# A transformer block and an RWKV block on one core: both ends of the program rebuilt, and all turn numbers replaced

## The reference

```python
# layer 0 (16 heads of 16), per batch
qkv = layernorm(x) @ w_qkv + b_qkv;  x = x + attention(q, k, v, mask_self) @ w_ao + b_ao
q = layernorm(x) @ w_q + b_q;  k, v = split(enc @ w_kv + b_kv);  x = x + attention(q, k, v, mask_cross) @ w_co + b_co
x = x + gelu(layernorm(x) @ w1 + b1) @ w2 + b2
# layer 1 (32 heads of 8)
xn = ln(x); sx = token_shift(xn); xxx = tanh((xn + sx * maa_x) @ maa_w1) @ maa_w2
x5 = xn + sx * (maa_stack + xxx)                       # five mixed streams
w = exp(-exp(time_decay + tanh(x5[1] @ decay_w1) @ decay_w2))
r, k, v, g = x5[3] @ Wr.T, x5[0] @ Wk.T, x5[2] @ Wv.T, silu(x5[4] @ Wg.T)
# over the tokens, per head: out_t = r_t (u k_t v_t + s);  s = k_t v_t + w_t s
x = x + groupnorm(out) * g @ Wo.T
xn2 = ln(x); sx2 = token_shift(xn2)
x = x + sigmoid((xn2 + sx2 * fmr) @ Wr2.T) * (square(relu((xn2 + sx2 * fmk) @ Wk2.T)) @ Wv2.T)
```

## Time and profile before

| | |
|---|---|
| median of three runs | 681.06 us |
| profiled execution, its span | 682.92 us, 681.1 us |
| first instruction of VectorE | 1.00 us |
| busy share PE, PEld, DVE, ACT, POOL | 94%, 82%, 88%, 84%, 46% |
| mean granted TensorE clock | 0.989 |
| granted clock in 653 to 659 us, in 659 to 660 us | 0.50 to 0.51, 0.58 |
| chain that ended last, by engine | PE 69%, ACT 16%, DVE 8%, issue 4%, DMA 1%, POOL 1% |
| PE idle in 0 to 17, 17 to 34, 34 to 51, 51 to 68 us | 6.5, 2.6, 2.6, 1.7 us |
| PE idle in 68 to 150 us, in 150 to 550 us | 3.0 us, 2.1 us |
| PE idle in 550 to 600, 600 to 640, 640 to 681.1 us | 6.2, 4.2, 11.2 us |

### The profile page before, as it was taken

One profiled execution on the slowest core, in us unless ns is written; L12 is line 12 of the kernel. 1 busy time (PEld: TensorE's weight loads), 2 busy tenths in 40 slices (PEclk: granted clock), 3 DMA queues, 4 the chain that ended last, 5 costly groups with the idle time before them and its releaser, 6 DMA issues.

```text
span 681.1 us, 17297 instructions
## 1 busy us (share of the span) xinstructions
PE 641.1 (94%) x5877; PEld 559.5 (82%) x5877; DVE 599.8 (88%) x1430; ACT 569.1 (84%) x2069; POOL 310.2 (46%) x440
## 2 busy tenths in 40 slices
PE   6889999999999999999999999999999989798876
PEld 5667788898888888988888888889889878688665
DVE  3699589999999999999999999999999997977674
ACT  1678999899999999999999999999999988664612
POOL 1254362546464554636364645446363644432220
PEclk9999999999999999999999999999999989999979
DMA  9920040310404050503122130505040222502200
GB/s 345 296 73 10 2 120 21 111 32 17 125 24 118 1 141 1 140 10 97 45 87 63 39 103 3 140 1 141 1 131 12 79 62 63 148 1 63 78 9 8
DMA packets 55293, 50.44 MB, mean 74 GB/s; under 512 B 6062, under 2 KB 50982, under 8 KB 54822
## 3 DMA queue, kind: packets, MB, share of 16 engines
q1 hardware_dynamic: 55206, 49.34, 24.8%
HBM read 28.62 MB, written 3.93 MB: 48 GB/s over the span
## 4 chain that ended last, share of the span: by engine, by line
PE 69%; ACT 16%; DVE 8%; issue 4%; DMA 1%; POOL 1%; SPq 0%; DVEq 0%; ACTq 0%
PE PS_B L730 14%; PE PS_T L832 8%; PE PS_S L730 6%; ACT SC L1473 5%; PE PS_B L872 5%; PE PS_D L737 5%; PE PS_T L840 4%; PE PS_S L803 4%; PE PS_S L737 3%; PE PS_T L737 3%; ACT PT L1483 2%; PE PS_D L978 2%; PE PS_D L730 2%; PE PS_T L723 2%; PE PS_B L894 2%
## 5 line engine op out<-in xcount | busy, mean ns | idle before, releaser
L1473 ACT ACTIVATE SC<-SC,NMX 128x128 f32<-128x128 f32 x512 | 200.1, 400 | 1.6 <-DVE NMX L1157 1.4
L1473 ACT ACTIVATION_READ_ACCUMULATOR SC<-SC,NMX 128x1 f32 x512 | 102.0, 199 | 0.0
L832 PE MATMUL PS_T<-CST,SC 128*128 128x128 f32 x512 | 81.0, 281 | 10.5 <-ACT SC L1473 6.2
L1157 DVE TENSOR_REDUCE NMX<-SC 128x4 f32<-128x512 f32 x128 | 84.1, 668 | 2.9 <-POOL SC L1680 1.9
L1483 ACT ACTIVATE PT<-PS_T 128x512 f32<-128x512 f32 x120 | 71.3, 594 | 11.5 <-PE PS_T L832 9.7
L832 PEld LDWEIGHTS PS_T<-CST,SC 128*128 128x128 f32 x512 | 56.6, 142 | 28.4 <-ACT PT L1483 14.7
L1238 DVE TENSOR_TENSOR_SCAN SS<-W,AJ 128x1024 f32<-128x1024 f32 x32 | 73.1, 2286 | 2.4 <-DMA W<-EW 1.7
L730 PE MATMUL PS_B<-MX,W 128*128 128x128 f32 x512 | 64.8, 276 | 1.1 <-ACT KR L1532 1.0
L1680 POOL TENSOR_TENSOR SC<-SC,MADD 128x512 f32<-128x512 f32 x48 | 60.1, 1278 | 6.9 <-DVE SC L1137 6.7
L730 PEld LDWEIGHTS PS_B<-MX,W 128*128 128x128 f32 x512 | 60.7, 192 | 1.8 <-ACT KR L1532 1.2
L730 PE MATMUL PS_B<-B_LT,W 128*128 128x128 f32 x512 | 61.2, 278 | 0.5 <-ACT B_LT L1411 0.4
(11 more groups left out here) (229 smaller groups left out, 1622.0 us busy)
## 6 DMA issues: line engine op xcount, KB each, us to landing
W<-EW SPq DMA_DIRECT2D x32, 512.0 KB, 4.1
V<-values_by_head SPq DMA_DIRECT2D x28, 512.0 KB, 5.7
W<-in_weights SPq DMA_DIRECT2D x1, 4160.0 KB, 18.1
ENC<-in_enc SPq DMA_DIRECT2D x16, 128.0 KB, 3.7
out<-X SPq DMA_DIRECT2D x16, 128.0 KB, 4.4
values_by_head<-VC SPq DMA_DIRECT2D x14, 128.0 KB, 2.1
X<-in_x SPq DMA_DIRECT2D x1, 1664.0 KB, 22.4
W<-in_weights SPq DMA_DIRECT2D x1, 1280.0 KB, 8.6
```

Of the source, the lines that this page charges most:

```text
L832: last = pe.transpose(PS_T[:, j * T:(j + 1) * T], SC[:, nr(b, a) % 2, g, j, :], ident)
L1157: dve.tensor_reduce(NMX[:, nr(b, a) % 2, GH * g:GH * g + GH], SC[:, nr(b, a) % 2, g], AX_X, ALU.max, negate=True)\
L1473: last = act.activation(SC[:, nr(b, a) % 2, g, j, :], SC[:, nr(b, a) % 2, g, j, :], ACT.Exp, bias=NMX[:, nr(b, a) % 2, h:h + 1], accum_out ...
```

## The change

The diff has six parts, and one that runs through everything.

1. **First statistics.** The load of the tokens gets a semaphore of its own (`in_tokens`), and VectorE takes the statistics and moments of batch 0 as soon as they are there, ahead of the tables. GpSimd makes `SEL` later, in `b_root(0, 0)`.
2. **Products on zeros.** GpSimd clears 128 columns of `A_N` first of all, and TensorE makes six products of these zeros ahead of its first wait. The products of the identity in front of `a_turn(0, 0)` go from 4 to 2, the two in front of `a_val(0, 0)` now stand in front of `a_key(0, 0)`, and those in `d_out(14)`, `d_val(14)` and `d_read(15)` are left out (two each).
3. **First values in a free bank.** The values of batch 0 go to `PS_B`, and `a_scores(0, 0)` no longer waits for them; every `a_pv` does.
4. **Row copies later.** The ScalarE copies of two bias rows (L1466) move from the first exponentials to behind the sixth.
5. **Last decays.** For batches 14 and 15 ScalarE writes the exponentials straight into `W8`, eight times over, in two activations of 128x1016; `b_wspread` issues nothing for them. `d_scan` waits for one half at a time.
6. **Last values in a free bank.** The value product of batch 15 goes to `PS_T` and no longer waits for the copy of keys and receptance; the gate product does.
7. **New turn numbers** for all engines and batches.

```diff
+EARLY_WARM = 6
-    ('a_turn', 0, 0): 4, ('a_val', 0, 0): 2, ('a_prob_turn', (0, 0), 0): 8, ('a_prob_turn', (0, 1), 0): 4,
+    ('a_turn', 0, 0): 2, ('a_key', 0, 0): 2, ('a_prob_turn', (0, 0), 0): 8, ('a_prob_turn', (0, 1), 0): 4,
...
-    ("a_turn", 0, 5845), ("a_val", 0, 7302), ("a_key", 0, 7410), ("a_query", 0, 7948), ("a_scores", 0, 9532),
+    ("a_turn", 0, 5768), ("a_key", 0, 6952), ("a_val", 0, 7612), ("a_query", 0, 7784), ("a_scores", 0, 9446),
...
-            sp.dma_start(X[:, 0, :], x[0]).then_inc(in_first, 16)
+            sp.dma_start(X[:, 0, :], x[0]).then_inc(in_tokens, 16)
...
+            pe.wait_ge(set_zero, 1)
+            for _ in range(EARLY_WARM):
+                pe.matmul(PS_B[:, 0, 0:P], A_N[:, 0:P], A_N[:, 0:P], start=True, stop=True)
             pe.wait_ge(in_first, IN_FIRST)
...
-                pe.wait_ge(a_v, nr(b, a) + 1)
+                pe.wait_ge(a_v, nr(b, a) + 1 if later(b, a) else 0)
...
             def b_valgate(b, k):
                 if k:
+                    if b == B - 1:
+                        pe.wait_ge(b_kr, B)
                     to_channels(PS_B[:, 0, C:2 * C], "g", C, 0, MX[:, 4]).then_inc(b_vgps, 1)
-                else:
+                elif b < B - 1:
                     pe.wait_ge(b_kr, b + 1)
                     pe.wait_ge(b_mx, 3 * b + 3)
                     to_channels(PS_B[:, 0, 0:C], "v", C, 0, MX[:, 2])
+                else:
+                    pe.wait_ge(a_res, 2 * B)
+                    pe.wait_ge(b_mx, 3 * B)
+                    to_channels(PS_T[:, 0:C], "v", C, 0, MX[:, 2]).then_inc(b_vgps, 1)
...
+            dve.wait_ge(in_tokens, 16)
+            dve.bn_stats(A_ST[:, :], X[:, 0, :]).then_inc(a_stat, 1)
+            dve.wait_ge(a_stat, 1)
+            dve.bn_aggr(A_MV[:, :], A_ST[:, :]).then_inc(a_var, 1)
             dve.wait_ge(set_col, 1)
...
                 act.wait_ge(b_w8, 32 * b)
-                act.activation(EW[:, :, 1:T], DW[:, :, 0:T - 1], ACT.Exp, scale=-1.0).then_inc(b_ew, 1)
+                if b < B - LAST:
+                    act.activation(EW[:, :, 1:T], DW[:, :, 0:T - 1], ACT.Exp, scale=-1.0).then_inc(b_ew, 1)
+                else:
+                    act.wait_ge(d_s, 2 * b)
+                    for t in range(CT):
+                        step = DW[:, t, 0:T - 1].unsqueeze(1).to_broadcast([P, RS, T - 1])
+                        act.activation(W8[:, t, :, 1:T], step, ACT.Exp, scale=-1.0).then_inc(b_w8, 16)
...
+            pool.memset(A_N[:, 0:P], 0.0).then_inc(set_zero, 1)
             pool.wait_ge(in_first, IN_FIRST)
-            pool.tensor_copy(SEL[:, :, :].rearrange("p d (h i) -> p d h i", i=RS),
```

More of the change, by code:

```diff
@@ new lines @@
+    ("b_mlp1", 0, 35991), ("b_mlp1", 1, 36020), ("b_mlp2", 0, 36342), ("b_mlp2", 1, 36691), ("b_turn", 1, 38299),
+    ("b_low1", 0, 39134), ("b_low2", 0, 39900), ("b_low2", 2, 40700), ("b_decay1", 0, 41270), ("b_decay2", 0, 42125),
+    ("b_keyrec", 0, 42323), ("b_keyrec", 1, 42364), ("b_valgate", 0, 42963), ("b_valgate", 1, 43267),
+    ("b_select", 0, 43467), ("b_select", 1, 44943), ("d_own", 0, 50288), ("d_read", 0, 50868), ("d_oturn", 0, 51334),
+    ("d_biasout", 0, 54082), ("d_yturn", 0, 54513), ("d_out", 0, 55700), ("d_turn", 0, 56815), ("d_keyrec", 0, 58592),
@@ new lines @@
+    ("b_valgate", 1): {0: 42756, 2: 42204, 9: 43545, 10: 42838, 11: 41952, 12: 43205, 15: 41878},
+    ("b_select", 0): {14: 44665, 15: 42269}, ("b_select", 1): {14: 47560},
+    ("d_own", 0): {0: 50406, 10: 50203, 14: 49416, 15: 42291}, ("d_read", 0): {0: 51208, 14: 50594},
+    ("d_oturn", 0): {4: 51277, 14: 50831}, ("d_yturn", 0): {0: 54056, 11: 54242, 13: 53492, 14: 51373},
+    ("d_out", 0): {10: 54980, 14: 52225}, ("d_keyrec", 0): {10: 58483, 13: 57612}, ("d_keyrec", 1): {10: 58507},
+    ("d_val", 0): {1: 59424, 2: 59414, 3: 59414, 4: 59414, 9: 59418, 10: 58511, 13: 59351},
@@ L767, in a_val @@
                         pe.wait_ge(in_wq, IN_WQ)
-                    to_tokens(values, "qkv", 3 * C, 2 * C, A_LT).then_inc(a_vps, 1)
+                    to_tokens(values if later(b) else first_values, "qkv", 3 * C, 2 * C, A_LT).then_inc(a_vps, 1)
             def a_key(b, a):
+                warm("a_key", a, b)
                 scores_read(pe, nr(b, a) - 1, 2)
@@ L1075, in a_stats @@
             def a_stats(b, a):
+                if not later(b, a):
+                    return
                 if a:
@@ L1235, in d_scan @@
                     dve.wait_ge(d_s0, b + 1)
+                    dve.wait_ge(b_w8, 32 * b + (32 if b < B - LAST else 16))
+                elif b >= B - LAST:
                     dve.wait_ge(b_w8, 32 * b + 32)
@@ L1430, in a_val @@
                 act.wait_ge(a_pvps, max(nr(b, a) - 1, 0))
-                v = values.rearrange("p (h q d) -> p h q d", q=2, d=HD)
+                made = values if later(b, a) else first_values
+                v = made.rearrange("p (h q d) -> p h q d", q=2, d=HD)
                 for q in range(2):
@@ L1462, in a_exps @@
                         .then_inc(set_bvt, 1)
+                if not later(b, a) and g == 1 and half == 0:
                     act.wait_ge(set_bo, 1)
```

473 lines of the change are left out of this document (270 added, 203 removed), and 8 rows, old and new, of the table PE_MOVED.

## The result

The changed kernel took 684.35 us (median of 16 executions, 681.91 to 687.93) against 681.50 us for the kernel before: ratio 1.0038, interval 1.0024 to 1.0052, some 2.6 us. (The ratio is the one that the interval belongs to; the two medians by themselves lie 2.85 us apart.) The difference is small but clear of the noise. 676.9 us was forecast, with a range up to 681.8. The profiled execution took 687.93 us, span 686.1 us; it was the slowest of the sixteen, so its trace shows some 3.6 us more than the median.

The account below looks back on a forecast made before the run. TensorE's work was taken to bound the steady part, waits and the clock the ends. Start -3.8, attention -1.1, batch 14 -0.2 and batch 15 +0.9 sum to -4.2 us: 681.06 becomes 676.9 us, range 672.8 to 681.8.

Parts of the forecast that it names:

- The start: First batch: earlier statistics, fast clock by the first queries and later row copies together give -3.8 us (bounds -0.6 and -4.8).
- row copies: ScalarE at the first exponentials: moving the copies leaves 1.25 us at PT, of which 0.3 is taken as gain.
- first rival: Start: the clock stays at the slow level, start -0.9, total -1.3, 679.8 us; chance 0.20.
- The steady part: Middle batches: the order changes, the work doesn't; 0 us, with bounds of -2 and +6.
- third rival: Steady batches: TensorE waits some 0.5 us once a batch for ScalarE or GpSimd, total +2.3, 683.4 us; chance 0.10.
- the prediction's own sign of being wrong: Span to the last attention's start doesn't shrink by 3 us, or the tail from there shrinks by more than 2.
- Batch 15's attention: Last attention: D_N ahead of AJ, XK products filling TensorE's 3.08 us wait; -1.1 us (bounds 0 and -3.1).
- Batch 14's decays: Batch 14's scan: the 1.68 us DMA stall goes, two ScalarE activations cost 1.6 more; -0.2 us (bounds -1.7 and +1.6).
- The rule of the Trainium skill: Last decays: issue a DMA early, wait late; by it alone part 5 would only cost, 1.6 us in each batch.
- Batch 15's decays and values: Last batch: VC, select and first scan come 1.6 us later; the read +0.9 us (bounds -1.9 and +2.7).
- `d_own`'s move: Between KK and the last read: `d_own` is done by then, where 1.85 us lay before.
- the rival of the dear end: End: batch 14's scan gains nothing, `d_own` saves nothing, the read runs slow (+1.0); total -1.2, 679.9 us; chance 0.14.

Follow-up runs that it names:

- e3_start: Parts 1 to 4 with new turn numbers below 35000 only, everything behind as in the kernel before; ratio to that kernel 0.9975, run again 0.9955.
- e1_after: The changed kernel once more, unaltered, for a second profile; ratio to the kernel before 1.0038.
- e5: The new start as in e3_start, with new turn numbers for everything below 165000 and the end as before; ratio to the kernel before 1.0053.
- x2_decays14: e3_start with the decays written by ScalarE for batch 14 alone; ratio to the kernel before 0.9955.
- x1: e3_start with the decays written by ScalarE for batches 14 and 15, run twice; ratios to the kernel before 0.9976 and 0.9974.

## Why the prediction was wrong, step by step

- **The start, -3.8 us: right in mechanism, less certain in size.** The statistics and the order did what was said, and TensorE was ready sooner: the zeros began at 0.98 us and took 2.93, CRAW's turn came at 3.84 (4.35 said), A_N at 5.44 (6.2 said). Scores were put at 12.1 us with the fast level and 15.05 with the slow one; they came at 11.3 and 13.7. Forecast and first rival both happen, from one execution to the next. The row copies were priced too low: I took 0.3 us of at most 1.25, but the lead grows by 1.3 us from the first scores to the second in every profile (1.91 to 3.20 us in the changed kernel, 4.30 to 5.60 in e3_start), and it has grown by the first PT already, 24.64 us before and 21.35 in the changed kernel. The lead at YT 1 is 2.5 us in the profiled execution, 4.9 in e1_after. Timed, the start alone gains 1.7 and 3.1 us, less than forecast.
- **The steady part, 0: the step that failed.** "Its order changes in some place of every batch, its work doesn't. With 0.5 us idle in 100 I put 0." The idle time only bounds what a new order can win; against a loss the 99.48% is no cover, since VectorE at 97% and ScalarE at 95% are nearly as full as TensorE. The new order loses 3.3 to 4.1 us against the kernel before in the nine steps between YT 1 and YT 10 (e5, e1 and the changed kernel), 0.4 us a batch on average: near the third rival, to which I had given 0.10, with its price of 0.5 and its 0.33 from which it decides. Its mechanism was right in part only. There isn't one wait per batch: TensorE's idle time grows by 2.2 us in 396, of which 1.3 are waits for QT, and its weight loads' by 5.9, and the loss of single batches goes from -0.3 to +1.7 us. And these new waits are for VectorE, not for ScalarE or GpSimd as the rival had it. Whether VectorE's own order or what feeds it makes them late stays open. By the prediction's own sign of being wrong, the span up to the last attention should have shrunk by 3 us; the product on XX in it came at 600.44 instead of 599.13 us.
- **Batch 15's attention, -1.1: didn't come.** The wait of 3.08 us for SC is gone, but with the products on XK first TensorE now waits 2.94 us for these, in the same place:

```profile
596.06 1.63 PE L824 MATMUL PS_D<-XK,W 128*128 128x128 f32 x8 [2.94 <-DVE XK L1485]
```

  I had taken XK to be ready. D_N did come first, but AJ behind it then waited 0.86 us for the DMA of the values, and the scan, the next norm's statistics and XK stand behind it:

```profile
590.87 1.22 DVE L1340 TENSOR_TENSOR AJ<-V,KR 128x1016 f32<-128x1016 f32 x1 [0.86 <-DMA V<-values_by_head]
```

  "To B_N" stayed at 120.81 us against 120.55, and that flatters the new order: the 120.55 have a fall of the clock in them, and kernels with the old order and no fall need 118.6 to 118.7.
- **Batch 14's decays, -0.2: right** (0.0 in x2_decays14). The rule of the Trainium skill that I weighed ("DMA: Bandwidth & Descriptors", "Rules for kernel authors") was the better guide for batch 15: there the DMA lay beside compute, and its replacement only cost (2.4 us to the read in the x1 profiles). For batch 14 it wasn't, as the 0.0 shows.
- **Batch 15's decays and values, +0.9: mis-sized, +2.3 us to the read in the profiled execution, because the clock was left out.** The activations took 1.99 us (2.0 said). From B_N to the first scan it is 23.70 us after and 20.89 before, 2.8 more: 1.6 are the activations, the other 1.2 are mainly YT (2.08 instead of 1.13 us) and the first half of select (2.21 us instead of half of 3.73), which run slow behind the 3.15 us pause. AJ ahead of XK added 0.9 (1.2 said), and from XK to the read 8.23 became 6.84 us: 1.4 less by `d_own`'s move (1.85 said). Sum +2.3, and the read itself at the slow level another 0.8, as the rival of the dear end had it: 3.1 us in the profiled execution, 1.9 in e1_after. That e1_after has just the forecast +0.9 to the read is luck: it was 3.5 us late at XK and won 2.6 back, 1.2 more than the changed kernel's other execution, with XK at the fast level (1.16 us).

Together, in the spans: -2.5 + 4.1 + 0.3 + 2.3 + 0.8 = +5.0 us (681.1 to 686.1). In e1_after: -4.9 + 3.7 - 0.4 + 0.9 + 0.9 = +0.2. The timed +2.6 lies between.

## What to carry to other kernels

Where three engines are each over 95% busy, as here, a new order of the steady part has little to win (0.5 us in 100) and more to lose (0.4 us a batch): price it by what the second engine has to spare, and look at every place where an engine loses the work that filled its wait for another. Take a start or an end rebuilt by hand without the new numbers for the rest; here the new start alone, with everything behind it as before, turned +2.6 into -1.7 and -3.1 us (the two runs of e3), and into -5.3 us with two pauses of TensorE filled. A wait of 3 us on TensorE can cost more than 3 us, since what follows may run at half the clock; an activation that replaces a hidden DMA can make just such a wait. And compare profiles only after looking at the level of the clock in each: the two of e3's kernel differ by 1.6 us at the first scores and by 1.6 more in the tail.
